# The last attention's sums by one product with ones for each key tile, inverted in all rows at once

## The reference, cut to what matters

```python
nx = _layer_norm(x, ln_gamma, ln_beta)
q = nx @ Wq
k = prototype_bank @ Wk
v = prototype_bank @ Wv
scores = jnp.einsum('bth,bph->btp', q, k) * H ** (-0.5)
weights = jax.nn.softmax(scores, axis=-1)
evidence = jnp.einsum('btp,bph->bth', weights, v)
...
return x + refined_delta
```

## Time and profile before

| | |
|---|---|
| median of 3 runs | 4512.72 us (4508.49 to 4527.49) |
| the profiled execution, its own time | 4508.28 us |
| its span in the profile | 4506.5 us |
| granted TensorE clock, share of full | 0.807 |
| busy over the span | PE 79%, PEld 35%, DVE 78%, ACT 66%, POOL 15% |
| last stage | from 2194 us on |
| DMA | 23.6% of 16 engines, 59 GB/s |

### The profile page before, as it was taken

How to read it: one execution, slowest core, us unless ns; L and a number is a source line. 1 busy time by engine, 2 the same in 40 slices (tenths; PEclk the granted TensorE clock), 3 DMA queues, 4 the chain that set the end, 5 groups by cost and what they waited for, 6 DMA issues and landing times.

```text
span 4506.5 us, 75222 instructions
## 1 busy us (share of the span) xinstructions
PE 3579.0 (79%) x28389; PEld 1586.2 (35%) x28389; DVE 3535.7 (78%) x5424; ACT 2958.1 (66%) x5488; POOL 695.1 (15%) x1464
## 2 busy tenths in 40 slices
PE   2679999986789999878476768778787877868788
PEld 2323333332323333233132334434343443434444
DVE  7658888937668888657699999898988989899532
ACT  1455888854647888838377776767767777676652
POOL 1322121104233333013011000010100001000000
PEclk8788999997879999978566676767777777677797
DMA  4553443204433333134301111011101101000000
GB/s 137 130 116 95 102 100 91 68 27 127 111 100 95 94 86 91 32 97 115 80 27 37 36 32 38 15 41 30 38 19 32 39 20 32 23 13 13 24 14 5
DMA packets 271170, 272.96 MB, mean 61 GB/s; under 512 B 38224, under 2 KB 245592, under 8 KB 270040
## 3 DMA queue, kind: packets, MB, share of 16 engines
q1 hardware_dynamic: 270808, 268.14, 23.6%
HBM read 145.99 MB, written 120.89 MB: 59 GB/s over the span
## 4 chain that ended last, share of the span: by engine, by line
DVE 21%; PE 17%; ACT 10%; issue 3%; POOL 0%; ACTq 0%; POOLq 0%; DVEq 0%
DVE m8b L2438 6%; DVE s_sb L2435 6%; ACT un L2038 5%; DVE s_sb L2441 5%; DVE mpart L2432 4%; PE xa_ps L1912 2%; PE xa_ps L1984 2%; PE ring L1828 2%; PE xa_ps L1934 2%; ACT prob L2111 2%; PE xa_ps L1917 2%; PE ring L1858 2%; ACT s_sb L2047 1%; PE e_ps L1870 1%; PE ring L1781 1%
## 5 line engine op out<-in xcount | busy, mean ns | idle before, releaser
L1415 DVE TENSOR_REDUCE mpart<-ring 128x1 f32<-128x400 f32 (+2 forms) x2816 | 1292.7, 523 | 233.8 <-PE ring L1204 230.8
L1333 ACT ACTIVATE prob<-xa_ps 128x512 f32<-128x512 f32 (+1 forms) x2048 | 1109.8, 595 | 239.8 <-PE xa_ps L1249 218.9
L2111 ACT ACTIVATE prob<-xa_ps 128x512 f32<-128x512 f32 (+1 forms) x832 | 451.9, 597 | 307.1 <-PE xa_ps L1917 241.3
L1204 PE MATMUL ring<-k_st,q_st 52*128 52x400 bf16 (+2 forms) x2560 | 579.4, 339 | 31.0 <-DVE mpart L1415 8.5
L1781 PE MATMUL ring<-k_st,q_st 52*128 52x400 bf16 (+1 forms) x1024 | 328.9, 441 | 295.4 <-ACT s_sb L2047 275.6
L1266 PE MATMUL xa_ps<-prob,va 128*9 128x256 f32 x6656 | 507.3, 384 | 0.4 <-ACT prob L1333 0.4
L2432 DVE MAX8 mpart<-s_sb 128x8 f32<-128x1601 f32 x256 | 456.2, 1817 | 54.2 <-ACT s_sb L2047 54.2
L2047 ACT ACTIVATE s_sb<-ring 128x400 f32<-128x400 f32 (+1 forms) x1024 | 468.2, 516 | 30.8 <-PE ring L1781 22.1
L2038 ACT ACTIVATE un<-s_sb 128x1601 fp8e4<-128x1601 f32 x256 | 392.9, 1535 | 136.9 <-DVE s_sb L2441 136.7
L2435 DVE MATCH_REPLACE8 s_sb<-mpart,s_sb 128x1601 f32<-128x1601 f32 x256 | 462.0, 1813 | 0.0
L2441 DVE MATCH_REPLACE8 s_sb<-m8b,s_sb 128x1601 f32<-128x1601 f32 x256 | 461.9, 1813 | 0.0
(11 more groups left out here) (304 smaller groups left out, 4155.3 us busy)
## 6 DMA issues: line engine op xcount, KB each, us to landing
k_st<-kc_dram SPq DMA_DIRECT2D x192, 300.2 KB, 5.4
o_dram<-o_sb SPq DMA_DIRECT2D x192, 128.0 KB, 1.8
kc_dram<-k SPq DMA_DIRECT2D x72, 300.0 KB, 3.2
ctx_t<-in_ctxT SPq DMA_DIRECT2D x24, 800.5 KB, 4.7
q_st<-q_dram SPq DMA_DIRECT2D x80, 192.0 KB, 4.0
kc_dram<-k SPq DMA_DIRECT2D x72, 200.0 KB, 3.6
k_st<-k_dram SPq DMA_DIRECT2D x48, 192.0 KB, 4.9
kc_dram<-k SPq DMA_DIRECT2D x24, 300.8 KB, 3.1
```

What stands on the lines that cost most here:

```text
L1204: nc.tensor.matmul(ring_ps[:, r % BANKS, 0:w], q_st[rows, b % NQ, 2 * t + pl, qt * P:(qt + 1) * P], k_st[rows, slot_of(n), pl, c0:c0 + w], ...
L1333: nc.scalar.activation(prob[0:size, s % NPROB, hf * 512:(hf + 1) * 512], x_ps[0:size, (2 * s + hf) % XBANKS, :], ACT.Exp, scale=HEAD_SCALE ...
L1415: nc.vector.tensor_reduce(mpart[:, n % 4, row, c:c + 1], ring_ps[:, r % BANKS, 0:chunks[c][1]], AX.X, ALU.max).then_inc(g["red"].sem, 1)
L2111: nc.scalar.activation(prob[0:size, s % NPROB, hf * 512:(hf + 1) * 512], x_ps[0:size, (2 * s + hf) % XBANKS, :], ACT.Exp, scale=HEAD_SCALE ...
```

## The change

The sums are made by one product for each key tile, in which ones [keys, 128] are stationary and the exponentials [keys, 256] move. Their result [128, 256] holds the sum of token c in all rows of column c, so `den3_ps` grows from 2 to 256 columns, the second half of the bank. VectorE inverts all of it, from PSUM to SBUF, into `rd3`, now a part of `hid`, and multiplies at the next step. The diagonal on GpSimd, the product with ones, the ring item rb, and ScalarE's copy are gone, with their semaphore. `evidence` moves from d + 58 to d + 55.

```diff
@@ -1507,9 +1507,8 @@
                 self.put(self.items, d + 39 + j, ("x3", b, j))
                 self.put(self.values, d + 41 + j, (b, j))
             self.put(self.recip, d + 54, b)
-            self.put(self.items, d + 57, ("rb", b))
-            self.put(self.out, d + 58, b)
-            self.end = d + 59
+            self.put(self.out, d + 55, b)
+            self.end = d + 56
         self.experts, self.stores = {}, {}
         self.weights = self.STEPS * B + 1
         for c in range(NC):
@@ -1627,14 +1626,13 @@
         ones3 = p.sb("ls_ones", [PARTS, P], BF16, ctx)
         negm = p.sb("ls_negm", [PARTS, T], BF16, ctx)
         prob3 = hid[:, 0:2, :]
-        rd3 = p.sb("ls_rd", [P, 2], F32, ctx)
-        diag3, rb = hid[:, 2, :], hid[:, 3, :]
+        rd3 = hid[:, 3, :]
         nx = p.sb("nx3", [P, TOK], F32, ctx)
         ring_ps = p.ps("ring", [P, BANKS, 512], ctx)
         xa_ps = p.ps("xa_ps", [P, XBANKS + 1, 512], ctx)
         x_ps, av_ps = xa_ps[:, 0:XBANKS, :], xa_ps[:, XBANKS, :].rearrange("p (u c) -> p u c", u=2)
         e_ps = p.ps("e_ps", [P, 512], ctx)
-        av3_ps, den3_ps = e_ps[:, 0:T], e_ps[:, T:T + 2]
+        av3_ps, den3_ps = e_ps[:, 0:T], e_ps[:, T:2 * T]
         block = ctx.enter_context(nc.Block())
         w3 = {n: p.w[:, W_OFF[3][0][n], :] for n in ("cq", "ck", "cv")}
         gate_co, gate_mlp = MOD_CROSS[2][2], MOD_MLP[2][2]
@@ -1817,12 +1815,9 @@
                 elif kind == "m2":
                     pe.wait_ge(g["red"].sem, g["red"].at(nth["m1b", b, NF - 1]))
                     pairs = [(weight(p, layer, "m2", f), hid[:, f, :]) for f in range(NF)]
-                elif kind == "q3":
+                else:
                     pe.wait_ge(g["h"].sem, g["h"].at(2 * b + 2))
                     pairs = [(w3["cq"], nx[:, tokens(b)])]
-                else:
-                    pe.wait_ge(g["diag3"].sem, g["diag3"].at(b + 1))
-                    pairs = [(p.const[:, C_ONES, :], diag3)]
                 ring_free(r)
                 for m, (w, v) in enumerate(pairs):
                     last = nc.tensor.matmul(out, w, v, start=m == 0, stop=m == len(pairs) - 1)
@@ -1868,9 +1863,7 @@
                 pe.wait_ge(g["rout"].sem, g["rout"].at(nth["x3", b, j]))
                 pr = prob3[0:sizes[j], j % 2, :]
                 nc.tensor.matmul(av3_ps[:], v3[0:sizes[j], j, :], pr, start=j == 0, stop=j == NT - 1, skip_group_check=True)
-                for h in range(2):
-                    last = nc.tensor.matmul(den3_ps[:, h:h + 1], pr[:, h * P:(h + 1) * P], p.const[0:sizes[j], C_ONES, 0:1], start=False, stop=j == NT - 1, skip_group_check=True)
-                last.then_inc(g["av3"].sem, 1)
+                nc.tensor.matmul(den3_ps[:], p.const[0:sizes[j], C_ONES, :], pr, start=False, stop=j == NT - 1, skip_group_check=True).then_inc(g["av3"].sem, 1)
 
             def ring_item(item):
                 r, kind = plan.at[item], item[0]
@@ -2065,13 +2058,11 @@
                     ins = nc.scalar.activation(v3[0:rows, 4 * i:4 * i + k, :], src[0:rows, 0:k * P].rearrange("p (k d) -> p k d", k=k), ACT.Copy)
                 elif kind == "t3":
                     ins = nc.scalar.activation(negm[:], src[0:PARTS, :].bitcast(BF16)[:, 0:T], ACT.Copy)
-                elif kind == "x3":
+                else:
                     n = b * NT + i
                     if n >= 2:
                         act.wait_ge(g["av3"].sem, g["av3"].at(n - 1))
                     ins = nc.scalar.activation(prob3[0:sizes[i], i % 2, :], src[0:sizes[i], 0:T], ACT.Exp, scale=float(D) ** -0.5)
-                else:
-                    ins = nc.scalar.activation(rb, src[:, 0:T], ACT.Copy)
                 ins.then_inc(g["rout"].sem, 1)
 
             def ring_out(item):
@@ -2249,11 +2240,6 @@
                 nc.gpsimd.tensor_tensor(mp3[:, :, 2], mx3[:], mp3[:, :, 1], ALU.subtract).then_inc(g["m3"].sem, 1)
                 done["m3"] = m + 4
 
-            def diagonal3(b):
-                pool.wait_ge(g["rden"].sem, g["rden"].at(b + 1))
-                nc.gpsimd.tensor_tensor(diag3.rearrange("p (k m) -> p k m", k=2), p.const[:, C_ID, :][:, None, :].to_broadcast([P, 2, P]),
-                                        rd3[:][:, :, None].to_broadcast([P, 2, P]), ALU.mult).then_inc(g["diag3"].sem, 1)
-
             nc.gpsimd.memset(ones3[:], 1.0).then_inc(g["zero"].sem, 1)
             for k in range(-1, STOP):
                 for n in chain_at.get(k, []):
@@ -2324,11 +2308,11 @@
 
             def recip3(b):
                 dve.wait_ge(g["av3"].sem, g["av3"].at(NT * (b + 1)))
-                nc.vector.reciprocal(rd3[:], den3_ps[:]).then_inc(g["rden"].sem, 1)
+                nc.vector.reciprocal(rd3, den3_ps).then_inc(g["rden"].sem, 1)
 
             def evidence(b):
-                dve.wait_ge(g["rout"].sem, g["rout"].at(nth["rb", b]))
-                nc.vector.tensor_tensor(p.o_all[:, tokens(b)], av3_ps, rb, ALU.mult).then_inc(g["ev"].sem, 1)
+                dve.wait_ge(g["rden"].sem, g["rden"].at(b + 1))
+                nc.vector.tensor_tensor(p.o_all[:, tokens(b)], av3_ps, rd3, ALU.mult).then_inc(g["ev"].sem, 1)
 
             def expert_begin():
 
```

More of the change, by code:

```diff
@@ L1544, in stage_last @@
     plan = Plan(True, NT, NCH, KU, VU, LEAD, 8, order)
-    BY_ACT = ("k", "v", "m", "s", "k3", "v3", "m1a", "q3", "t3", "x3", "rb")
+    BY_ACT = ("k", "v", "m", "s", "k3", "v3", "m1a", "q3", "t3", "x3")
     plan.count(BY_ACT)
@@ L1555, in stage_last @@
         + [f"{s}{i}" for s in ("k", "q", "mrow", "ost") for i in range(4)] + [f"{s}{i}" for s in ("nl", "rl") for i in range(2)])}
-    g.update({s: p.sig("ls_" + s) for s in ("loaded", "bias", "lx", "top", "m3", "mchain3", "av3", "rden", "diag3", "ev")})
+    g.update({s: p.sig("ls_" + s) for s in ("loaded", "bias", "lx", "top", "m3", "mchain3", "av3", "rden", "ev")})
     g.update({s: p.sig("n_" + s) for s in ("sq", "rv", "rstd", "diag", "h")})
@@ L2268, in _ @@
                     chain3(b)
-                for b in order.recip.get(k, []):
-                    diagonal3(b)
                 for item in items.get(k, []):
@@ L2448, in stage_last @@
               "recip": B, "out": B, "zero": 2, "rs0": 16 * B // 2, "rs1": 16 * B // 2, "ctx": 16 * len(loads), "loaded": 32, "bias": 2, "lx": 2 * B, "top": B, "m3": B,
-              "av3": B * NT, "rden": B, "diag3": B, "ev": B, "sq": 2 * B, "rv": 2 * B, "rstd": 2 * B, "diag": 2 * B, "h": 2 * B}
+              "av3": B * NT, "rden": B, "ev": B, "sq": 2 * B, "rv": 2 * B, "rstd": 2 * B, "diag": 2 * B, "h": 2 * B}
     for i in range(4):
```

## The result

| | us |
|---|---|
| before, median of 3 | 4512.72 (4508.49 to 4527.49) |
| changed, median of 3 | 4456.24 (4449.99 to 4457.76) |
| ratio, 95% interval | 0.9864 (0.9826 to 0.9902) |
| profiled execution, its own time and its span | 4449.99 and 4448.2 |
| granted clock over the span | 0.824, before 0.807 |

The change saves 56 us by the medians; by the ratio of all executions it is 1.4%. The forecast was 4511 with a range down to 4484, so it is wrong. The faster rival had the direction, but even its lower end, 4467, lies above what was measured.

The account below looks back on a forecast made before the run. TensorE was taken to bound the attention phases, VectorE the stretches between; 10.4 + 2.1 + 3.4 + 7.6 - 1.8 - 0.8 = +20.9 us, less 18 for the clock, +2.9 on 4508.28: 4511 us, range 4484 to 4540.

Parts of the forecast that it names:

- The faster rival: The clock also rises in group 7's loop: -13.5 us there, 4491 us in all, 4467 with phases at their bound; chance 0.24.
- The pair's price: Each key tile's new sums' product costs more than the four old ones: +0.26 us at half clock, +0.12 at full.
- my +3.4 us for group 7: In group 7's loop, 13 tiles, all at half clock, each pay 0.26 us more for the sums: +3.4 us.
- The clock: In the phases of groups 0 to 5 full-width products raise the granted clock to about 0.81: -18 us.
- my +2.9: Net change for the whole kernel: +20.9 us without the clock, less 18 us that the clock gives back.
- The slope: Attention phases shorten by 6 us for 0.15 more of the granted clock, taken from groups 0 and 1.
- My bound for this term: The most the clock gives back in groups 0 to 5: phases down to 62 us, -42 us.
- The slower rival: The clock does not move, so groups 0 to 5 pay for products and reciprocal: +20.9 us, 4529 us; chance 0.24.
- Hidden anyway: Pipeline slack takes both costs and the clock stays: 4513 us; chance 0.52 together with the forecast.
- The reciprocal: VectorE inverts 256 columns, not 2: 1750 ns, +1.59 us each, +7.6 us at the start of six stretches between phases.
- What goes: Diagonal, broadcast product and copy disappear after the sums: -1.8 us over six groups, and less in group 7's tail.
- the bare tail: After group 7's last product, the reciprocal alone replaces reciprocal, diagonal, product and copy, 2.59 us: -0.8 us.

Follow-up runs that it names:

- experiments 10 to 12: Changed kernel with the sums' product cut to 128 columns (4435.9 us), in bfloat16 (4442.23 us), and in bfloat16 with five more products before group 7's loop (4440.11 us).
- Experiment 8: Kernel before, with the new full-width sums' product in group 7 alone: 4500.94 us, ratio 0.996.
- experiment 1: Kernel before, plus an unread 254-column product for each key tile: 4483.65 us, ratio 0.9949; run again for a second profile, 4502.19 us.
- experiment 6: The changed kernel once more, unaltered: 4454.77 us, ratio 0.9856.
- Experiment 5: Changed kernel with the old one-column products and a reciprocal of 2 columns, the broadcast left out: 4512.6 us, ratio 0.999.
- experiment 3: Changed kernel with the sums' product moving one column for key tiles 1 to 12: 4473.63 us, ratio 0.9903.
- experiment 10: Changed kernel with the sums' product cut to 128 of 256 columns for key tiles 1 to 12: 4435.9 us, ratio 0.9816.

## Why the prediction was wrong

**What bounds the kernel** was read rightly: TensorE in the phases, VectorE between them, TensorE alone in group 7. The phases moved; the stretches did not become shorter.

**The pair's price** (+0.26 us at half clock, +0.12 at full) was mis-sized: it is 0.85 us at half and 0.43 at full, so +0.14, and +0.07 to +0.09 by which row of the old four is taken. L1870, my model, was the wrong one. It takes 1.01 us to the next start because its own first weights come late: in the changed kernel the load of L1865 begins with the product (both 4383.31), while that of L1866 begins at 4383.90, 0.42 us ahead of its product. The sentence of the Trainium skill (TensorE: Matmul & The Clock Gate, "Step-by-step: what each phase is for"), that the next tile's weights load during this tile's matmul, which I set aside for L1870's row, holds for the new pair; for L1865 itself it fails, which again takes 4384.32 - 4383.31 = 1.01 us. In group 7 the product with the keys behind the sums gave the price back, so at half clock there was none: 3.18 us before and after. Of my +3.4 us for group 7 nothing came.

**The clock** is the step that failed. I let it rise from 0.735 to 0.81 in groups 0 to 5, which was to give back 18 us by a slope between two phases that were both bound by TensorE, and in group 7 I let it stay at half. In groups 0 to 5 it went to 0.85 to 0.91, and the phases became 47 us shorter, with the products' own price in it, where my two terms for that (+10.4 and -18) made 7.6. In group 7 it rose to 0.83 and the loop became 13.5 us shorter, where I had +3.4. Group 6 became 5 us shorter, where I had +2.1, with 0.92 of the clock in place of 0.84. Against the forecast the three came out 39, 17 and 7 us shorter; the span missed my +2.9 by 61 us, and the stretches and the end nearly cancel. The slope was too flat as well: group 1's phase went from 68 us at 0.81 to 62 at 0.91, 6 us for a step of 0.10, where I had taken 6 for 0.15. An estimate with my slope, the measured clock (0.895 in the mean) and the measured price gives about 32 of the 47 us. A chain in which L1872 has 7.5% showed what the instruction costs, not what its shape does to everything beside it.

My bound for this term was summed wrongly. Six phases of 62 us are 372, 51 under the 423 of before, and with +10.4 for the products the clock would have had to give back 61 us for that, not 42. With 61 the faster rival's lower end would have been 4448, and the measured time would have been inside it. What stopped the gain near 62 us is not shown. VectorE is close (56.4 us busy), but TensorE's lines lead the chain of the phase, and with less work for TensorE and the same for VectorE most phases came to 60 or 61 us (experiments 10 to 12).

**The faster rival** had group 7 right, a rise after some tiles. That its -13.5 us is also what was found is in part luck: it had the clock rise after three tiles and a longer tile until then, and the clock rose in the second and the tile was no longer. Experiment 8 gives 19 us for it alone by the medians. I gave the rival 0.24, and what I set against it was a tile that becomes longer, 3.44 us. In experiment 1 each tile has the same wide product and the four one-column products behind it (4.03 us, 4432.15 to 4436.18 in its timeline), and its loop stayed at half in both profiles. So the wide product alone did not bring the rise there; that the one-column products were gone belongs to it.

**The slower rival** fell: the clock moved. **Hidden anyway** fell too.

**The reciprocal** was right in duration (1743 ns for 1750). Its price is not settled. The stretches grew by 9 us in the profile above, forecast 7.6, but in the changed kernel's second profile (experiment 6) they take 1165 us, against 1166 before. The Trainium skill's repeat count of 8 (VectorE: DVE Perf Modes, "First, the fixed hardware budget") gave an estimate of 2.1 us for it; the trace disagrees, with 1743 ns or 6.3 ns a column.

**What goes:** the bare tail saved 0.80 us, forecast 0.8. The end behind the last loop is 2.8 us shorter; its clock is 0.90 and was 0.84, which I had counted only in the faster rival, with 3 us. Experiment 5 shows the shorter way as a whole at nothing that can be measured (0.999).

What stays open is what in the change brings the clock. Experiment 1's second profile has all four one-column products and the wide one, and 0.84 to 0.92 in the phases; experiment 3 has two one-column products and nothing wide in their place, and 0.70 to 0.83; before has 0.66 to 0.81. So both the wide product and the one-column products that are gone seem to have a part, and their shares are not measured. I did not try a kernel with the old loads' length and no change of the clock.

## What to carry to other kernels

A product with one moving column isn't cheap only because it is short: the four took 0.36 to 0.71 us here, the wide pair 0.43 to 0.85. Where TensorE is the bound and its granted clock is between the levels, try the operands the other way round, so that constants are stationary and the data move. Price such a change twice, once for its instructions and once for what the clock does to every product around it, and take the work of the next engine as the far bound of the second, here VectorE's 56 us under phases of 60 to 65. Then try less of the added work too, as experiment 10's 128 columns, which had the same clock here.

## What the runs showed of the hardware

- More work made the program faster (experiment 1: 0.9949). I had thought of the clock as a bonus that softens a cost.
- The granted clock of the same work differs within one execution: before, the phases of groups 0 to 5 have 0.66 to 0.81 and take 65 to 75 us. The times of one program can lie in two bunches, experiment 1's ten at 4474 to 4485 and 4510 to 4532 us; why is not shown.
- The clock rose in group 7 in the midst of a TensorE that was busy without a break by the profile's measure, before and after. The busy share (4.00 of 4.00 us in both kernels) doesn't tell the two apart: by that measure a stretch with one-column products is as busy.
- A pair of equal products takes 1.01 or 0.85 us at half clock, the same 256 columns side by side in one tile. The load of the first one's weights begins with it in the one case and 0.42 us ahead of it in the other.
